# Loop heads of an attention kernel on the first slot of an instruction fetch block

## Chip, cores and metric

One Trainium2 chip, one core of it. The metric is the device time of one launch in microseconds (us), the median over several runs; lower is better. Four compute engines matter: TensorE (PE; its weight loads are listed as PEld), VectorE (DVE), ScalarE (ACT) and GpSimd (POOL). SyncE (SP) issues DMAs. Each engine runs its own instruction stream, and the streams meet at semaphores.

## What is computed

The input x is 4 x 2048 x 512 in float32. After a layernorm, `xn`, three things are added up:

```python
x = x + attention(xn) + tanh(xn @ weight @ aux_weight1 @ aux_weight2 + bias)
```

The attention has 16 heads of 32 channels: q, k and v from 512x512 weights with biases, `softmax(q k^T / sqrt(32)) v` over 2048 keys, and an output projection with its bias. With 4 batches there are 64 pairs of batch and head. They are called heads from here on, h = 0 to 63.

## The kernel before

The kernel has three stages, each in a block of its own. `build_weights` turns and multiplies the weights, `build_project` makes q, k, v and the tanh branch for 16 blocks of 512 tokens and stores them in DRAM, and `build_attend` works through the 64 heads and then makes the output projection. The projections and the scores hold their operands as a high and a low part, for accuracy; the stacks of three parts of 32 rows give the 96-row operands in the trace.

A head in `build_attend` has 16 key tiles (kt) of 128 keys and 4 query blocks (q) of 512, so 64 units.

- PE makes, for each unit, a tile of scores for the row maximum of the next head (`max_scores`, L837, into `sm_bank`) and a transposed tile of scores of this head (`scores`, L853, into one of three buffers of `st_bank`). After every second key tile it multiplies two finished tiles of exponentials by v (`use`, which calls `spread`, L859, into `pv_bank`). Once per head it adds up the softmax denominators (`add_up`, also L859, into `sum_bank`).
- DVE takes the row maxima out of `sm_bank` (`maxima`, L773).
- ACT takes the exponentials out of `st_bank` (`exps`, L695) and issues the DMAs that load q, k and v of the head three ahead (`load`, L210 for the q and k parts). With three buffers in `st_bank`, PE can be three units ahead of it.
- POOL adds ten of the sixteen tiles of exponentials in nine additions (`add`, L641), issues the five accumulating DMAs that add the other six (`join`, L652: 1 MB each, each waiting for the one before), and scales a result (`scale`, L659). The place of a tile of exponentials is used again once its addition or its join is done; ACT waits for that.
- SP spreads the reciprocals and stores the context.

What sets the order is written out by hand: `body(h, r, more, following)` of each engine handles key tiles 6 to 15 of head h and then key tiles 0 to 5 of head h + 1 (on POOL: the additions of head h + 1). The helper `heads` runs it. Its loop (`Fori`, the `with` line at L508) has 15 trips of four heads, r = 0 to 3, and the last four heads are written out behind the loop. The loop runs on each engine by itself, with a counter and a closing branch of its own, so an engine goes round without a barrier. [...] One trip holds about 2,660 instructions on PE, 715 on ACT, 540 on DVE, 190 on POOL and 100 on SP, register and wait instructions included and the two instructions of a matmul (weight load and matmul) counted as two. Before the loop, each engine's stream holds the other stages and the first pieces of head 0, so the loop's first instruction falls on whatever slot of a fetch block comes next.

Of the kernel before, what the change touches and what calls it, by code (L numbers as in the profile page):

```python
# [29 lines left out]
ALL_HEADS = BATCH * HEADS  # L30
GROUP = 4
# [421 lines left out]
def build_attend(nc, dram, out, first):  # L453
# [3 lines left out]
    with ExitStack() as own:  # L457
# [47 lines left out]

        def heads(eng, body):

            with nc.Fori(0, ALL_HEADS // GROUP - 1, engines=[eng.engine], hint_back_edge=True) as i:  # L508
                after = eng.snap(i + 1)
                for r in range(GROUP):  # L510
                    body(i * GROUP + r, r, GROUP, after * GROUP + (r + 1 - GROUP))
            for r in range(GROUP):
                body(ALL_HEADS - GROUP + r, r, GROUP - 1 - r, ALL_HEADS - GROUP + r + 1)
# [17 lines left out]
        def _(sp):  # L531
# [49 lines left out]
            def body(h, r, more, following):  # L581
# [16 lines left out]
                elif more == 1:  # L598
                    load_y(0, 0)

            heads(sp, body)
            store_result(1, 1)
            load_y(3, 1)
# [16 lines left out]
        def _(pool):  # L620
# [48 lines left out]
            def body(h, r, more, following):  # L669
                for i in range(POOL_ADDS):  # L670
                    if i == SCALE_ADD:
                        scale(h, r)
                    if more >= 1:
                        sum_up(following, (r + 1) % GROUP, i)

            heads(pool, body)

        @block.scalar
        def _(act):
# [45 lines left out]
            def body(h, r, more, following):  # L725
# [11 lines left out]
                else:  # L737
# [4 lines left out]
                    copy_sums(h, r)  # L742

            heads(act, body)
            for n in range(2, 4):
                high(n, n % 2)
# [255 lines left out]
```

## Time and profile before

| | us |
|---|---|
| time, median of 3 runs | 4283.07 (4282.47 to 4283.51) |
| profiled execution, its own time | 4286.54 |
| its span, first to last instruction | 4284.8 |
| PE busy | 4171.0 (97%) |
| POOL busy | 3185.7 (74%) |
| DVE busy | 2932.3 (68%) |
| ACT busy | 2361.2 (55%) |

The profile is of one execution. Its times count from the first instruction. "Busy" leaves out register, branch, wait and DMA-issuing instructions. An engine's name with a q (ACTq) is its sequencer. A wait put down to "issue" is one in which the engine waited for nothing that the profile shows. [...] Names such as `probs` and `sm_bank` are the program's; `probs` and `dma_sum` are both tiles of exponentials.

### The profile page before, as it was taken

The numbers are of one execution on the slowest core, as the hardware profiler recorded it, in microseconds if no ns is written. First come the engines' busy times: TensorE is split into PE (matmuls) and PEld (weight loads), VectorE is DVE, ScalarE is ACT, GpSimd is POOL, SyncE is SP. The second block draws the span as 40 slices with busy tenths as digits, with TensorE's granted clock in tenths as the row PEclk, the third lists the DMA queues.
The fourth block names the chain that finished last, engine by engine and source line by source line (L and its number), as shares of the span: only waits on it lengthen the run. The fifth ranks groups of instructions, "written<-read, shape, count | busy, mean of one in ns | idle before, by whom it ended". The sixth has DMA issues, their size and how long they took to land.

```text
span 4284.8 us, 77480 instructions
## 1 busy us (share of the span) xinstructions
PE 4171.0 (97%) x21728; PEld 2535.4 (59%) x21728; DVE 2932.3 (68%) x4928; ACT 2361.2 (55%) x4517; POOL 3185.7 (74%) x1119
## 2 busy tenths in 40 slices
PE   7999999999999999999999999999999999999999
PEld 5888888655555555555555555555555555555467
DVE  4344334488787777878777878787777878787434
ACT  2222222056676666666666667666666667666621
POOL 0322222279899999999999999999999999899930
PEclk9999999899999999999999999999999999999999
DMA  4444445357777777777777777777777777777677
GB/s 155 147 169 164 147 157 177 127 107 159 150 154 146 154 155 151 158 150 157 153 151 151 155 150 160 148 157 149 153 150 156 152 155 153 152 154 154 150 243 256
DMA packets 268281, 673.43 MB, mean 157 GB/s; under 512 B 109056, under 2 KB 110080, under 8 KB 214656
## 3 DMA queue, kind: packets, MB, share of 16 engines
q0 software_dynamic: 46080, 335.56, 41.1%
q1 hardware_dynamic: 138784, 220.26, 15.7%
q10 hardware_dynamic: 83040, 113.01, 9.5%
q8 instruction: 184, 3.01, 0.3%
q14 instruction: 193, 1.58, 0.1%
HBM read 195.30 MB, written 137.36 MB: 78 GB/s over the span
## 4 chain that ended last, share of the span: by engine, by line
PE 68%; issue 4%; POOL 3%; ACT 2%; DMA 2%; DVE 1%; ACTq 0%; POOLq 0%; DVEq 0%
PE pv_bank L859 21%; PE sm_bank L837 21%; PE st_bank L853 20%; POOL pool_sum L641 3%; PE sm_bank L200 3%; ACT probs L695 2%; PE sm_bank L859 2%; DMA dma_sum<-probs 1%; DVE part_max L773 1%; PE st_bank L200 1%; DMA q_stack<-max_row 1%; PE sm_bank L846 0%; DMA s_sums<-sum_copy 0%; POOL dma_sum L652 0%; ACTq L694 0%
## 5 line engine op out<-in xcount | busy, mean ns | idle before, releaser
L773 DVE TENSOR_REDUCE part_max<-sm_bank 128x1 f32<-128x512 f32 x4096 | 2498.4, 682 | 633.4 <-PE sm_bank L837 633.1
L641 POOL TENSOR_TENSOR pool_sum<-pool_sum,probs 128x2048 f32<-128x2048 f32 x512 | 2453.6, 4792 | 75.0 <-ACT probs L695 61.5
L695 ACT ACTIVATE probs<-st_bank 128x512 f32<-128x512 f32 x3840 | 1960.1, 617 | 679.5 <-PE st_bank L853 596.3
L853 PE MATMUL st_bank<-q_stack,k_stack 97*128 97x512 f32 x4096 | 1650.6, 404 | 66.3 <-ACT probs L695 58.4
L837 PE MATMUL sm_bank<-k_stack,q_stack 96*128 96x512 f32 x4096 | 1691.5, 417 | 11.4 <-DVEq L751 9.4
L837 PEld LDWEIGHTS sm_bank<-k_stack,q_stack 96*128 96x128 f32 x4096 | 786.9, 192 | 557.6 <-DVE part_max L773 323.4
L853 PEld LDWEIGHTS st_bank<-q_stack,k_stack 97*128 97x128 f32 x4096 | 780.4, 191 | 343.5 <-ACT probs L695 188.1
L859 PE MATMUL pv_bank<-probs,v_pair 128*32 128x512 f32 x7680 | 959.2, 615 | 0.0
L859 PEld LDWEIGHTS pv_bank<-probs,v_pair 128*32 128x32 f32 x7680 | 207.3, 111 | 467.7 <-ACT probs L695 274.0
L652 POOL DMA_DIRECT2D dma_sum<-probs x320 | 300.0, 938 | 150.8 <-DMA dma_sum<-probs 148.6
L312 POOL TENSOR_TENSOR y_out<-y_out,x_in 128x512 f32<-128x512 f32 x64 | 82.7, 1292 | 370.3 <-ACT y_out L341 364.4
L641 POOL TENSOR_TENSOR pool_sum<-probs 128x2048 f32<-128x2048 f32 x64 | 311.1, 4861 | 52.6 <-ACT probs L695 52.5
L385 DVE SCALAR_TENSOR_TENSOR qk_lo<-proj,qk_bias,qk_hi 128x512 fp32r<-128x512 f32 x128 | 96.2, 751 | 206.7 <-ACT qk_hi L335 205.0
L335 ACT ACTIVATE qk_hi<-proj,qk_bias 128x512 fp32r<-128x512 f32 x128 | 88.2, 689 | 264.8 <-PE proj L200 264.8
L695 ACT ACTIVATE dma_sum<-st_bank 128x512 f32<-128x512 f32 x256 | 132.5, 603 | 172.7 <-PE st_bank L853 172.7
L341 ACT ACTIVATE y_out<-y_out 128x512 f32<-128x512 f32 x64 | 40.5, 632 | 325.6 <-DVE y_out L407 325.6
L305 POOL TENSOR_TENSOR rstd<-rstd,power 128x4 f32<-128x4 f32 x16 | 16.3, 1018 | 260.2 <-DVE rstd L363 260.2
L200 PE MATMUL proj<-xt_hi,w_hi 128*128 128x512 f32 x512 | 203.7, 398 | 1.5 <-DVE xt_lo L375 1.5
L200 PE MATMUL proj<-w_hi,xt_lo 128*128 128x512 f32 x512 | 203.8, 398 | 0.0
L200 PE MATMUL proj<-xt_lo,w_hi 128*128 128x512 f32 x512 | 203.6, 398 | 0.0
L200 PE MATMUL proj<-xt_hi,w_lo 128*128 128x512 f32 x512 | 203.4, 397 | 0.0
L200 PE MATMUL proj<-w_hi,xt_hi 128*128 128x512 f32 x512 | 202.4, 395 | 0.0
(88 smaller groups left out, 2324.9 us busy)
## 6 DMA issues: line engine op xcount, KB each, us to landing
dma_sum<-probs POOLq DMA_DIRECT2D x320, 1024.0 KB, 8.5
q_stack<-s_q_hi ACTq DMA_DIRECT2D x122, 256.0 KB, 5.4
k_stack<-s_k_hi ACTq DMA_DIRECT2D x122, 256.0 KB, 5.2
x_in<-in_x SPq DMA_DIRECT2D x16, 1024.0 KB, 7.8
s_q_hi<-qk_hi SPq DMA_DIRECT2D x16, 1024.0 KB, 4.3
s_q_lo<-qk_lo SPq DMA_DIRECT2D x16, 1024.0 KB, 6.4
s_k_hi<-qk_hi SPq DMA_DIRECT2D x16, 1024.0 KB, 4.3
s_k_lo<-qk_lo SPq DMA_DIRECT2D x16, 1024.0 KB, 6.4
```

The source lines that it names most:

```text
L200: last = nc.tensor.matmul(out, a(c), b(c), start=(c == 0 and n == 0), stop=(c == CT - 1 and n == 2))
L312: nc.gpsimd.tensor_tensor(y_out[:, j], y_out[:, j], x_in[:, par, j], ALU.add).then_inc(half_y, 1)
L335: nc.scalar.activation(qk_hi[:, t, g], proj[:, u % RING], ACT.Identity, bias=keep["qk_bias"][:, t, g:g + 1]).then_inc(hi_ready, 1)
L341: nc.scalar.activation(y_out[:, j], y_out[:, j], ACT.Tanh).then_inc(tanh_ready, 1)
L385: nc.vector.scalar_tensor_tensor(qk_lo[:, t, g], proj[:, u % RING], keep["qk_bias"][:, t, g:g + 1], qk_hi[:, t, g].bitcast(F32), ALU.add, ...
L641: nc.gpsimd.tensor_tensor(total[:], one[:], tile_at(r, kt)[:], ALU.add).then_inc(pool_added, 1)
L652: nc.gpsimd.dma_start(dma_sum[c][r % 2][:], tile_at(r, CHAINS[c][j])[:], accum_op=ALU.add).then_inc(joined[c], DMA)
L695: nc.scalar.activation(tile_at(r, kt)[:, q * BLK:(q + 1) * BLK], st_bank[:, st_place(kt * QB + q)], ACT.Exp, scale=SCALE).then_inc(probs_r ...
L773: nc.vector.tensor_reduce(part_max[:, k:k + 1], sm_bank[:, sm_place(k)], AX.X, ALU.max).then_inc(max_scores_read, 1)
L837: nc.tensor.matmul(sm_bank[:, sm_place(k)], q_st[r][0:ROWS, q * P:(q + 1) * P], k_st[r][0:ROWS, b * BLK:(b + 1) * BLK], start=True, stop=T ...
L853: nc.tensor.matmul(st_bank[:, st_place(u)], k_st[r][0:ROWS + 1, kt * P:(kt + 1) * P], q_st[r][0:ROWS + 1, q * BLK:(q + 1) * BLK], start=Tr ...
L859: last = nc.tensor.matmul(bank[q * DH:(q + 1) * DH, :], left, right[:, q * BLK:(q + 1) * BLK], start=start, stop=stop)
```

## The change

The loop in `heads` gets one more argument. The library then pads each engine's stream ahead of the loop, so that the loop's first instruction is loaded at slot 0 of a fetch block. The padding is branched over, once, when the loop is entered. The body of the loop, its hint, its waits and the code behind it are the same instructions in the same order, only at other slots.

```diff
@@ build_attend, heads @@
 
         def heads(eng, body):
 
-            with nc.Fori(0, ALL_HEADS // GROUP - 1, engines=[eng.engine], hint_back_edge=True) as i:
+            with nc.Fori(0, ALL_HEADS // GROUP - 1, engines=[eng.engine], hint_back_edge=True,
+                         head_slot={eng.engine: 0}) as i:
                 after = eng.snap(i + 1)
                 for r in range(GROUP):
                     body(i * GROUP + r, r, GROUP, after * GROUP + (r + 1 - GROUP))
```

## Rows read from the trace of the kernel before

**Rows 1.** The page: span and engines

```profile
span 4284.8 us, 77480 instructions
PE 4171.0 (97%) x21728; PEld 2535.4 (59%) x21728; DVE 2932.3 (68%) x4928; ACT 2361.2 (55%) x4517; POOL 3185.7 (74%) x1119
```

**Rows 2.** The loop's own line, all trips: first and last start of each instruction

```profile
L508 PEldq BRANCH_PREFETCH_HINT  x15: 36/36/50, 888.8 to 3703.9; - x15
L508 ACTq BRANCH_PREFETCH_HINT  x15: 40/40/50, 888.8 to 3706.6; - x15
...
L508 PEldq COMPARE_BRANCH  x15: 88/357/387, 1084.1 to 3904.6; - x15
```

**Rows 3.** Stretches on PE: trip one, trip two, trip three

```profile
core 0: us, PE busy (x) PEld busy (x) DVE busy (x) ACT busy (x) POOL busy (x), PEclk, DMA share, GB/s
888.80:1084.10 195.30, 194.62 (x1088) 108.84 (x1084) 159.04 (x269) 134.88 (x265) 184.39 (x59) 1.00 0.73 155
1084.50:1285.90 201.40, 197.35 (x1096) 109.58 (x1092) 158.28 (x268) 134.96 (x264) 186.93 (x61) 0.98 0.73 153
1285.90:1488.00 202.10, 197.47 (x1100) 109.26 (x1092) 158.26 (x269) 134.93 (x264) 186.83 (x61) 0.98 0.73 153
```

**Rows 4.** Waits of ACT and of PE, loop (871 to 3910 us)

```profile
ACT probs L695 <- issue: 54.5, 14, 4.3
...
PE st_bank L853 <- ACT probs L695: 52.9, 16, 4.2
```

**Rows 5.** Waits of all engines, first trip (871 to 1084 us)

```profile
ACT probs L695 <- POOL pool_sum L641: 0.5, 1, 0.5
...
PE st_bank L853 <- ACT probs L695: 0.3, 2, 0.2
```

**Rows 6.** The loop's line around the second back-edge (1284 to 1294 us)

```profile
L508 ACTq COMPARE_BRANCH  x1: 59/59/59, 1288.7 to 1288.7; - x1
L508 ACTq BRANCH_PREFETCH_HINT  x1: 40/40/40, 1289.1 to 1289.1; - x1
```

**Rows 7.** Timeline of ACT behind that back-edge

```profile
1289.43 1.57 ACT L695 ACTIVATE probs<-st_bank 128x512 f32<-128x512 f32 x3 [0.25 <-PE st_bank L853]
1290.78 0.34 ACTq L210 DMA_DIRECT2D q_stack<-s_q_hi  x1
1290.88 0.62 ACT L695 ACTIVATE probs<-st_bank 128x512 f32<-128x512 f32 x1
1295.82 2.08 ACT L695 ACTIVATE probs<-st_bank 128x512 f32<-128x512 f32 x4 [4.32 <-issue]
```

**Rows 8.** Timeline of PE behind it; the last row is undisturbed, for comparison

```profile
1296.46 0.80 PE L853 MATMUL st_bank<-q_stack,k_stack 97*128 97x512 f32 x1 [4.19 <-ACT probs L695]
1297.19 3.64 PE L859 MATMUL pv_bank<-probs,v_pair 128*32 128x512 f32 x16
...
1267.13 1.92 PE L859 MATMUL pv_bank<-probs,v_pair 128*32 128x512 f32 x16
```

**Rows 9.** Stretches around that back-edge, with the granted clock

```profile
1280.00:1290.00 10.00, 9.93 (x63) 5.06 (x55) 6.09 (x11) 5.30 (x11) 10.00 (x4) 1.00 0.53 107
1290.00:1296.40 6.40, 2.28 (x10) 1.20 (x8) 3.86 (x7) 2.08 (x6) 6.32 (x2) 0.84 0.72 146
1296.40:1300.90 4.50, 4.43 (x18) 1.03 (x18) 0.00 (x0) 1.50 (x4) 4.29 (x3) 0.50 0.61 127
```

**Rows 10.** DMA queues in the second full trip of ACT (1288.7 to 1489.5 us)

```profile
q8 instruction: 11, 0.18, 0.4%
q14 instruction: 12, 0.10, 0.1%
```

**Rows 11.** DMA issues in the first trip: the joins

```profile
dma_sum<-probs POOLq DMA_DIRECT2D x20, 1024.0 KB, 8.5
```

**Rows 12.** Waits of POOL in the 14 later trips (1084 to 3906 us)

```profile
POOL dma_sum L652 <- DMA dma_sum<-probs: 128.9, 56, 4.0
POOL pool_sum L641 <- ACT probs L695: 58.9, 49, 3.5
```

**Rows 13.** Waits of ACT in the heads behind the loop (3906 to 4120 us)

```profile
ACT probs L695 <- issue: 1.9, 1, 1.9
ACT probs L695 <- POOL pool_sum L641: 1.8, 1, 1.8
```

**Rows 14.** Timeline of POOL around the second back-edge

```profile
1286.63 1.21 POOL L652 DMA_DIRECT2D dma_sum<-probs  x1
...
1305.90 4.59 POOL L641 TENSOR_TENSOR pool_sum<-pool_sum,probs 128x2048 f32<-128x2048 f32 x1 [3.29 <-ACT probs L695]
...
1331.81 0.88 POOL L652 DMA_DIRECT2D dma_sum<-probs  x1 [4.00 <-DMA dma_sum<-probs]
```

## The prediction

> **What bounds the kernel now.** The page comes first: PE is busy for 97% of the span and no other engine for more than 74% [rows 1]. In a kernel where PE alone is nearly full, moving instructions to other slots can save only what PE loses while it waits or while its clock is down. So the question is whether anything in the trace repeats with the loop.
>
> The second view is the line of the loop itself. The hint is the first instruction of a trip and the closing branch the last. On PE the first branch starts at 1084.1 us and the fifteenth at 3904.6 us [rows 2], so fourteen trips take 2820.5 us, or 201.46 us each. The first trip, entered from above and not by the branch, takes from 888.8 to 1084.1 us, 195.3 us, for the same body; with the 0.4 us that a taken branch needs on PE [rows 2] that is 195.7. Stretches cut at these times show the same: the clock is at 1.00 all through trip one and at 0.98 in trips two and three, and DVE, ACT and POOL have as much work in each [rows 3]. Every trip that is entered by the taken branch costs 5.8 us more than the one that is not.
>
> The third view says where. In the loop, ACT waits 14 times for "issue", 54.5 us in all, and PE waits 52.9 us for ACT's exponentials [rows 4]; 14 is the number of taken branches. In trip one the first of these is absent and the second is 0.3 us [rows 5]. The timeline behind the second back-edge gives the order: ACT's branch starts at 1288.7 and its hint runs at 1289.1 [rows 6], so the branch itself costs 0.4 us. ACT then does four exponentials and one DMA and stops until 1295.82, with 4.32 us of wait for nothing the trace shows [rows 7]. PE, at most three units ahead, stops with it: 4.19 us before its next score matmul. [...]
>
> What ACT waits for is, I think, its own instructions. Two queues carry only instructions, and in a trip they make 11 and 12 transfers, of 16 KB (0.18 MB / 11) and of 8 KB (0.10 MB / 12) [rows 10], so no engine that needs many of them keeps the loop. [...]
>
> [...] The trace puts 0.4 us at the branch and the long wait five operations behind it. [...]
>
> **The change part by part.** The head moves to slot 0 on five engines.
> - ACT: a whole block lies behind the branch instead of a remainder. Twelve loads of 8 KB a trip for some 1,250 instructions of ACT and DVE make a block some 105 instructions, about a seventh of ACT's trip, near 30 us, against the 6.8 us from hint to resumption (1289.1 to 1295.82). The wait goes, and with it PE's wait and the half clock: 5.8 us a trip if nothing else is late.
> - What is late next is POOL. In the fourteen later trips it waited 58.9 us for ACT [rows 12], nearly all of it right behind the back-edge (3.29 us in one piece, [rows 14]). That is 4.2 us a trip in which it caught up. Without it POOL's own trip is 201.46 - 4.2 = 197.25 us, of which 128.9 / 14 = 9.2 us are waits for its joins [rows 12]. ACT cannot write a tile of exponentials before POOL or a join has done with the old one, so a POOL that falls behind holds ACT, and PE with it. Bounds: 195.7 us a trip if POOL's lag stays free, 197.25 if POOL paces. In trip one, which had no rest for POOL either after its first additions, ACT was held for 0.5 us [rows 5]. I take 0.5 us over PE's pace, 196.2, because trip one is the nearest row.
> - DVE, POOL, SP: nothing waits for instructions in their streams now, and each keeps a first block longer than or equal to what it has. POOL's 190 and SP's 100 instructions are one or two blocks. Cost nothing; the cover is DVE's slack, 158 us busy in a trip of 201 [rows 3], and if its target came late PE would wait for its maxima as it now waits for ACT.
> - PE: the body is 2,660 instructions in 11 loads, ten full blocks and about 100 instructions, 7.6 us at the pace of the trip. [...] Nothing shows what this costs; from below it is 0; from above it is a join's 8.5 us less 7.6, 0.9, and as much again for the load itself, about 2 us. I take 0, since PE shows no such wait today, and keep the 2.
> - Entry: one taken branch over the padding per engine, 0.4 us once. The code behind the loop also moves; it has one such wait of 1.9 us on ACT [rows 13], which could go or double: plus or minus 2 us.
>
> The sum: 14 x (201.46 - 196.2) = 73.6, less 0.4, is 73.2 us. The profiled execution took 4286.54 us (span 4284.8), 3.5 us over the median; on it the sum gives 4213.3, and on the median of 4283.07 it gives **4210 us**.
>
> **The rivals.**
> - A, PE alone paces: 195.7 a trip, 80.7 - 0.4 saved, 4203 us. For it: ACT was held by POOL for only 0.5 us in trip one. Against it: the four last heads, which have no back-edge, show 1.8 us of that wait [rows 13].
> - B, POOL paces from the second trip on: 197.25, 59 us saved, 4224 us. For it, the 4.2 us of rest that disappear; against it, that a join's wait can shrink when POOL starts it at another time.
 Against it: today's branch on PE costs 0.4 us in every trip, with the same hint.
> - E, the wait has another cause (a fetch that every taken branch pays), or the head is not moved on ACT: 4283 us. [...]
>
> **How the numbers follow.** Forecast 0.46, A 0.18, B 0.16, C 0.08, D 0.04, E 0.08. The first four are faster, 0.88. A difference under 0.2% (8.6 us) can't be told from no change in this kernel; E lies there, 0.08, and D gives slower, 0.04. The range takes in A with 5 us for the code behind the loop and for trips that differ, 4198, and C nearly whole, 4236.
>
> **What would show it.** In the profile of the changed kernel: ACT's "issue" wait of 14 times gone or down to single ones; the branch-to-branch time on PE at 196 us instead of 201.5; the granted clock at 1.00 through the loop; PE's 3.64 us groups gone. For POOL: its wait for ACT shrinks from 58.9 us to under 20, and ACT's wait for POOL grows, little by the forecast, to over 10 us by B. C or D would show as PE starting its hint later than 0.4 us behind its branch. The prediction is wrong if a wait of over 3 us stays behind ACT's back-edge, or if PE's trip comes out above 198 us.

## The result, and the profile after

The changed kernel takes 4232.77 us (median of 4 runs, 4230.62 to 4234.31); the kernel before took 4282.77 us beside it (4 runs, 4275.68 to 4283.51). The ratio is 0.9884, with a 95% interval of [0.9873, 0.9896]; a bracket behind a ratio is this interval below too. It is faster by 50 us, where 73 us were forecast. The profiled execution took 4234.31 us, against 4286.54 us in the profile of before. In the fences below each line number behind line 508 is one higher than in the rows of before.

The page of the changed kernel, span and engines; they answer to [rows 1]. Below them is the page's part 4, the chain of work that ended last, by engine.

```profile
span 4232.5 us, 77485 instructions
PE 4144.6 (98%) x21728; PEld 2528.2 (60%) x21728; DVE 2932.1 (69%) x4928; ACT 2359.9 (56%) x4517; POOL 3189.9 (75%) x1119
...
PE 55%; DMA 9%; issue 7%; POOL 6%; ACT 3%; DVE 1%; POOLq 0%; ACTq 0%; SPq 0%; DVEq 0%
```

The same line of the page of the kernel before:

```profile
PE 68%; issue 4%; POOL 3%; ACT 2%; DMA 2%; DVE 1%; ACTq 0%; POOLq 0%; DVEq 0%
```

PE has 26 us less busy time, although it does the same 21,728 matmuls: the stretches at half clock (0.50 in [rows 9]) are gone. The chain runs through PE less, and more through transfers (9% where it was 2%) and through POOL (6% where it was 3%). That is the first sign of what paces the kernel now.

The loop's own line in the changed kernel, with instruction count, shortest, median and longest duration in ns, and first and last start; it answers to [rows 2]. The branch counts 16 because the entry is now a taken branch too.

```profile
L508 PEldq COMPARE_BRANCH  x16: 88/734/1908, 886.6 to 3846.0; - x16
...
L508 PEldq BRANCH_PREFETCH_HINT  x15: 36/36/50, 887.0 to 3649.9; - x15
```

The branches that close the trips start at 1084.7 us (first) and 3846.0 us (fifteenth) on PE, so the fourteen trips between them take 2761.2 us by the unrounded times, 197.23 us each instead of 201.46. The first trip is longer than it was, 1084.7 - 887.0 = 197.7 us against 195.3. And PE's branch itself, 0.36 us in the median before, now takes 0.73 us and up to 1.91 us.

Stretches on PE of the changed kernel (columns as in [rows 3]; PEclk is the clock granted to TensorE, as a share of the full one): trip one, the fourteen later trips, and the 20 us around the second back-edge, which answer to [rows 3, 9].

```profile
887.00:1084.70 197.70, 195.45 (x1096) 108.93 (x1092) 158.71 (x268) 134.57 (x264) 184.46 (x58) 1.00 0.72 153
1084.70:3845.90 2761.20, 2734.06 (x15284) 1522.36 (x15280) 2216.49 (x3752) 1887.37 (x3696) 2622.77 (x841) 1.00 0.74 156
1280.00:1300.00 20.00, 19.96 (x115) 10.35 (x113) 15.11 (x26) 13.17 (x27) 19.84 (x7) 1.00 0.70 140
```

The granted clock is 1.00 in all three. Around the back-edge, where PE was busy for 2.28 us of 6.4 and then ran at 0.50 [rows 9], it is now busy for 19.96 us of 20.

The timeline of ACT in the changed kernel behind the second back-edge, which answers to [rows 7]:

```profile
1285.13 1.57 ACT L696 ACTIVATE probs<-st_bank 128x512 f32<-128x512 f32 x3 [0.24 <-PE st_bank L854]
1286.49 0.34 ACTq L210 DMA_DIRECT2D q_stack<-s_q_hi  x1
1286.58 2.09 ACT L696 ACTIVATE probs<-st_bank 128x512 f32<-128x512 f32 x4
```

The three exponentials and the DMA are those of [rows 7]; the fourth exponential now runs on into the fifth, where ACT used to stand still for 4.32 us.

Waits in the fourteen later trips of the changed kernel (1084.7 to 3846 us): total us, times, longest. They answer to [rows 4, 12].

```profile
POOL dma_sum L653 <- DMA dma_sum<-probs: 116.6, 71, 4.5
...
PEld st_bank L854 <- DMA q_stack<-max_row: 24.7, 24, 1.5
PE st_bank L854 <- DMA q_stack<-max_row: 18.4, 26, 1.1
ACT probs L696 <- DMA dma_sum<-probs: 10.1, 7, 2.1
...
PE st_bank L854 <- ACT probs L696: 2.8, 4, 0.9
POOL pool_sum L642 <- ACT probs L696: 2.7, 4, 1.0
ACT probs L696 <- POOL pool_sum L642: 1.8, 1, 1.8
```

The same waits in the kernel before, over its fourteen later trips (1084.1 to 3905 us), those that [rows 4, 12] don't hold:

```profile
ACT probs L695 <- POOL pool_sum L641: 5.2, 3, 1.8
PEld st_bank L853 <- DMA q_stack<-max_row: 1.2, 3, 0.7
PE st_bank L853 <- DMA q_stack<-max_row: 0.4, 1, 0.4
```

ACT's 54.5 us of "issue" are gone altogether, PE's 52.9 us for ACT (52.6 of them in these trips) are down to 2.8, and POOL's 58.9 us for ACT to 2.7. One wait has come in their place: PE, and its weight loads, wait for `q_stack<-max_row`, 18.4 and 24.7 us where it was 0.4 and 1.2. That is the 8 KB transfer with which SP writes the next head's row of maxima into the query stack (`load_row`).

What such a wait looks like can be read in the changed kernel's timeline of POOL, SP and PE around one end of a head:

```profile
2933.09 0.88 POOL L653 DMA_DIRECT2D dma_sum<-probs  x1
2933.71 9.55 POOL L642 TENSOR_TENSOR pool_sum<-pool_sum,probs 128x2048 f32<-128x2048 f32 x2
...
2937.86 0.54 SPq L541 DMA_DIRECT2D q_stack<-max_row  x1
...
2943.20 0.86 POOL L653 DMA_DIRECT2D dma_sum<-probs  x1
...
2944.40 0.50 PE L854 MATMUL st_bank<-q_stack,k_stack 97*128 97x512 f32 x1 [0.86 <-DMA q_stack<-max_row]
```

POOL issues the third join of a head at 2933.09; by the trace it lands 9.3 us later. SP issues the row 4.8 us behind it, while the join is under way, and PE, whose next scores need the row, gets it at 2944.40, 6.5 us after its issue and 0.86 us too late. Meanwhile POOL makes two additions, 9.55 us, and issues the fourth join at 2943.20.

Put together, on PE's own marks: 14 x (201.46 - 197.23) = 59.2 us are won in the later trips, 2.4 us lost in the first and 6.4 us behind the loop (386.5 us from the last branch to the end, against 380.1). A rest of 1.8 us was won ahead of the loop. Together that is 52.2 us, against 52.3 us between the two spans.

### The profile page after: what moved, and what is told of

Read it like the earlier page. It is cut to its first block, busy times and chain, and to the rows that moved or that the text cites. A ratio compares the mean times of both kernels' runs of the same rounds, so it can differ in the third digit from the quotient of the medians.

```text
span 4232.5 us, 77485 instructions
## 1 busy us (share of the span) xinstructions
PE 4144.6 (98%) x21728; PEld 2528.2 (60%) x21728; DVE 2932.1 (69%) x4928; ACT 2359.9 (56%) x4517; POOL 3189.9 (75%) x1119
## 4 chain that ended last, share of the span: by engine, by line
PE 55%; DMA 9%; issue 7%; POOL 6%; ACT 3%; DVE 1%; POOLq 0%; ACTq 0%; SPq 0%; DVEq 0%
PE pv_bank L860 17%; PE sm_bank L838 16%; PE st_bank L854 16%; POOL pool_sum L642 5%; DMA dma_sum<-probs 5%; DMA q_stack<-max_row 3%; ACT probs L696 3%; PE sm_bank L200 2%; PE sm_bank L860 2%; DVE part_max L774 1%; PE st_bank L200 1%; DMA q_stack<-s_ctx 0%; PE sm_bank L847 0%; POOL dma_sum L653 0%; DVE max_row L758 0%
## 5 line engine op out<-in xcount | busy, mean ns | idle before, releaser
L860 PE MATMUL pv_bank<-probs,v_pair 128*32 128x512 f32 x7680 | 935.4, 602 | 0.0
```

The costliest lines, as they stand in the source:

```text
L860: last = nc.tensor.matmul(bank[q * DH:(q + 1) * DH, :], left, right[:, q * BLK:(q + 1) * BLK], start=start, stop=stop)
```

## The experiments

The times below were each taken beside the kernel before. "Trip" is the mean of the fourteen later trips on PE and "branch gaps" the sum over them of the time from PE's branch to the hint behind it; both are worked out from the loop's line, and were 201.46 and 6.0 us before and 197.23 and 15.7 us after. All edits are made to the changed kernel.

### Which engine's slot does it

ACT alone aligned:

```diff
-                         head_slot={eng.engine: 0}) as i:
+                         head_slot={eng.engine: 0} if eng.engine == mybir.EngineType.Activation else None) as i:
```

> Only ACT's loop head is put on slot 0; the other four keep the slots of the kernel before. Theory (ACT ran out of its block behind the branch, and joins and row loads pace what is left): the wait for issue behind ACT's back-edge is gone, the trip on PE is 197.2 us as with all five aligned, PE's branch is back at 0.36 us median instead of 0.73, the time is 4233 us, within 5 us. Rival (another engine's alignment carries part of it): the time stays above 4250 us.

Measured: 4217.86 us (4215.12 to 4220.05), ratio 0.9839 [0.9823, 0.9855]; trip 196.80, branch gaps 6.1, 379.7 us behind the loop. Every engine but ACT aligned (the two arms of the condition swapped):

> Slot 0 for PE, DVE, POOL and SP, while ACT's head keeps its old slot. Theory: the 3.9 us wait behind each of ACT's fourteen back-edges stays, and the time is that of the kernel before, 4283 us, up to 10 us more for PE's slower branch. Rival: under 4270 us.

Measured: 4282.99 us, 0.9996 [0.9987, 1.0006]; trip 200.95, branch gaps 16.6.

Waits of ACT in the later trips (1085 to 3900 us) with all engines but ACT aligned:

```profile
ACT probs L696 <- issue: 44.2, 13, 4.2
```

So the whole gain is ACT's. The four other engines bring none, and together with ACT they take away 15 us of it, which neither theory had: both had ACT alone at about 4233 us or above. ACT alone was run once more, beside the last experiment below:

> The kernel with ACT's head alone at slot 0 once more, in more rounds and beside the two above: 4218 us. If the 15 us to the kernel with all five aligned were chance, it comes out at 4225 to 4233 us.

Measured: 4218.25 us (4216.3 to 4223.45), 0.9852 [0.9839, 0.9866]; trip 196.69. Its interval lies clear of that of all five (0.9873 to 0.9896), so the 15 us stand. It is the fastest version here that computes everything.

### Is it the length of ACT's first block

ACT's head at slot 111, the others at 0:

```diff
-                         head_slot={eng.engine: 0}) as i:
+                         head_slot={eng.engine: 111 if eng.engine == mybir.EngineType.Activation else 0}) as i:
```

> All heads at slot 0 but ACT's at slot 111, 17 slots ahead of a multiple of 128. If ACT's blocks hold 128 instructions (8 KB), it runs dry after 17 instructions and the wait of some 3.9 us comes back fourteen times: trip 201.5 us, time 4283 to 4290 us. If its blocks hold 256 instructions, 145 slots are left, over 30 us of work, and the time is that of all at slot 0, 4233 us.

Measured: 4282.06 us, 0.9985 [0.9973, 0.9997]; trip 201.18.

Timeline of ACT behind the second back-edge, with ACT's head at slot 111:

```profile
1288.64 0.34 ACTq L210 DMA_DIRECT2D q_stack<-s_q_hi  x1
1288.72 0.62 ACT L696 ACTIVATE probs<-st_bank 128x512 f32<-128x512 f32 x1
1292.40 2.08 ACT L696 ACTIVATE probs<-st_bank 128x512 f32<-128x512 f32 x4 [3.06 <-issue]
```

ACT's wait in its later trips (1085 to 3900 us) in the same kernel:

```profile
ACT probs L696 <- issue: 38.3, 12, 4.2
```

The stall of the kernel before is back, at the same operation and at nearly the same cost (201.18 us a trip, 201.46 before). The theory with blocks of 128 had said so, 201.5 us. In a block of 256 instructions slot 111 would leave 145 of them behind the head, more than the 32 that were enough at slot 96 below, and nothing would happen; so the run decides for blocks of 128, of which 17 are left. Such a block goes with the transfers of 8 KB: 12 of them a trip for some 1,250 instructions of ACT and DVE [rows 10], some 105 each by the prediction's estimate, where blocks at the ends of a trip need not be used whole.

When is the block behind the target asked for: as the engine enters the target's block, or once that is used up? ACT's head at slot 96 leaves 32 instructions:

```diff
-                         head_slot={eng.engine: 0}) as i:
+                         head_slot={eng.engine: 96 if eng.engine == mybir.EngineType.Activation else 0}) as i:
```

> All heads at slot 0 but ACT's at 96, with 32 slots left in its block instead of 17. Undisturbed, ACT reaches the 32nd instruction 6.5 us behind its hint, and in the kernel before it went on 6.8 us behind it. Theory: the wait shrinks to 0.5 us or nothing, no half clock, trip 197.2 to 197.5 us, 4233 to 4238 us. Rival (the next block is asked for only when the block is used up): the wait of 3.9 us stays, 4283 us.

Measured: 4233.06 us, 0.9884 [0.9869, 0.9899]; trip 197.63. From 871 to 3860 us ACT has no "issue" wait at all, where it had 12 (38.3 us) with its head at slot 111. If the fetch began only at the block's last instruction, the wait would have been there at slot 96 too. So it begins earlier, and 32 instructions of ACT's work cover it.

### Does PE's short last block cost the rest

PE's 2,660 instructions a trip go with 11 transfers of 16 KB [rows 10]; at ACT's 8 KB for 128 instructions each holds 256, an estimate. By it, with PE's head at slot 128, its last block in the loop has some 230 instructions instead of some 100:

```diff
-                         head_slot={eng.engine: 0}) as i:
+                         head_slot={eng.engine: 128 if eng.engine == mybir.EngineType.PE else 0}) as i:
```

> PE's head at slot 128, the others at 0. PE's last block then holds 231 instructions ahead of the branch instead of 103, some 17 us instead of 7.6. Theory (the load of the target sometimes comes late behind a join): PE's branch falls from a median of 0.73 us to 0.36 us. Whether the time follows tells who paces the trip: PE, then some 0.4 us a trip less, 6 us in all, 4227 us; joins and row loads, then no change, 4233 us.

Measured: 4236.41 us (4230.07 to 4244.51), 0.9891 [0.987, 0.9911]; trip 197.33, branch gaps 5.9. The times spread over 14 us, so a few us either way would not show in them.

The loop's line on PE, with PE's head at slot 128:

```profile
L508 PEldq COMPARE_BRANCH  x16: 88/357/391, 888.6 to 3846.6; - x16
```

Waits in its later trips (1085 to 3838 us):

```profile
POOL dma_sum L653 <- DMA dma_sum<-probs: 108.8, 67, 3.5
...
ACT probs L696 <- DMA dma_sum<-probs: 18.7, 9, 2.7
PE st_bank L854 <- DMA q_stack<-max_row: 14.1, 23, 1.3
```

PE's branch is back to 0.36 us, and the 9.8 us that it had gained in gaps are gone. The trip and the time have not moved. So PE's late branch was real and cost nothing that can be measured. That PE would otherwise have waited for the row of maxima instead fits these rows, but is argued and not shown by itself.

### What paces the trip now

The joins are the 1 MB accumulating transfers that POOL issues, and POOL waits for them. If their length has a part in the pace, halving them frees it; if PE's own work set it, nothing would move. This kernel leaves out half of the columns in every sum that a join makes:

```diff
-                nc.gpsimd.dma_start(dma_sum[c][r % 2][:], tile_at(r, CHAINS[c][j])[:],
+                nc.gpsimd.dma_start(dma_sum[c][r % 2][:, :SEQ // 2], tile_at(r, CHAINS[c][j])[:, :SEQ // 2],
```

> All five heads at slot 0; the five joins of a head move half of each tile, 512 KB instead of 1 MB, so the other half of those sums is left out. Theory (the joins' durations pace POOL, and their traffic delays the row loads): the trip on PE falls from 197.2 us to PE's own 195.7 to 196.1 us, PE's waits for the row load (46 us in the loop) fall under 10 us, the time is 4205 to 4215 us. Rival (POOL's own additions pace): the trip stays above 196.8 us.

Measured: 4193.89 us, 0.9786 [0.9769, 0.9804]; trip 195.16, first trip 194.1, 375.8 us behind the loop.

DMA issues of the kernel with half joins, later trips (1086 to 3830 us): count, KB each, median us from issue to landing.

```profile
dma_sum<-probs POOLq DMA_DIRECT2D x281, 512.0 KB, 4.9
q_stack<-max_row SPq DMA_DIRECT2D x56, 8.0 KB, 2.0
```

Its waits (1085 to 3838 us):

```profile
POOL pool_sum L642 <- ACT probs L696: 90.3, 57, 2.0
POOL dma_sum L653 <- DMA dma_sum<-probs: 10.4, 13, 1.3
```

The same two DMA issues in the changed kernel (1086 to 3830 us):

```profile
dma_sum<-probs POOLq DMA_DIRECT2D x279, 1024.0 KB, 8.6
q_stack<-max_row SPq DMA_DIRECT2D x56, 8.0 KB, 5.4
```

With joins of 4.9 us PE no longer waits for the row of maxima (the row is in none of its waits), POOL again waits for ACT instead of for its joins, and the trip is 195.16, under the 195.7 that stood in the prediction for PE's own pace. The time is 11 us below the lower end of what was expected. The 8 KB row takes 5.4 us to land beside 1 MB joins and 2.0 us beside halved ones. The edit takes away two things at once, POOL's waits for joins and the late row, so by itself it does not tell which of them paced; the next two kernels look at them one by one.

Rival B had POOL pace by its own work. Then less addition would speed it up. This kernel adds only half the columns in one of POOL's additions of each head, and leaves out the other half:

```diff
-                nc.gpsimd.tensor_tensor(total[:], one[:], tile_at(r, kt)[:], ALU.add).then_inc(pool_added, 1)
+                w = slice(0, SEQ // 2 if i == 5 else SEQ)
+                nc.gpsimd.tensor_tensor(total[:, w], one[:, w], tile_at(r, kt)[:, w], ALU.add).then_inc(pool_added, 1)
```

> All five heads at slot 0; the sixth of POOL's nine additions adds half the columns, so a part of the sum is left out and POOL has about 2.3 us a head less to do; the joins stay whole. Theory (POOL's additions plus joins are one chain that paces the trip): the chain is 9 us a trip shorter, POOL waits for ACT again, the trip falls to 195.7 to 196.1 us and the time to 4205 to 4215 us. Rival (the row load alone paces, because any join in flight delays it): PE's waits for the row load stay over 25 us in the loop and the trip above 196.8 us.

Measured: 4227.41 us, 0.9865 [0.9848, 0.9883]; trip 197.35, first trip 194.1.

Waits in its later trips (1085 to 3838 us):

```profile
POOL dma_sum L654 <- DMA dma_sum<-probs: 241.9, 111, 4.5
...
PE st_bank L855 <- DMA q_stack<-max_row: 15.9, 26, 1.1
```

Its timeline of POOL between a third and a fourth join, one addition narrow:

```profile
2930.30 7.35 POOL L643 TENSOR_TENSOR pool_sum<-pool_sum,probs 128x1024 f32<-128x1024 f32 x2
2939.96 0.88 POOL L654 DMA_DIRECT2D dma_sum<-probs  x1 [2.31 <-DMA dma_sum<-probs]
```

A miss. The addition became shorter and the trip did not: POOL's wait for its joins grew from 116.6 to 241.9 us and swallowed what was freed. But this shows less than that POOL's additions don't matter, for the addition that was narrowed is one of the two that run beside the third join, the longest (9.9 us in the mean). In the changed kernel, over the later trips, the five stretches from one join's issue to the next take 10.46, 10.09, 10.54, 8.53 and 9.70 us in the mean, 49.3 us a head. In the first, second and fifth POOL waits for next to nothing (0.01 us): its additions fill them. Ahead of the fourth join it waits 0.39 us for the third, and ahead of the fifth 1.79 us for the fourth. With the narrow addition the wait ahead of the fourth join is 2.60 us, and the stretch 10.58; the other four are unchanged within 0.02 us. So additions and joins stand one behind the other in POOL's round, and an addition that a join hides cannot shorten it. Whether a shorter addition in one of the other three stretches would, no run tried. The rival of that expectation, that the late row alone paces, had both its signs here: PE and its weight loads still waited 37 us for the row, and the trip was above 196.8.

Is the row of maxima only in the way, so that asking for it earlier wins the time? It is asked for four units of maxima earlier with

```diff
-TURN_UNIT = 8
+TURN_UNIT = 4
```

> All five heads at slot 0; the row of maxima is turned at unit 4 of the next head instead of unit 8, so its 8 KB load starts about one key tile (3 us) earlier, and nothing else changes. If the late row load is what paces PE: the waits for it vanish and the trip falls to 196.0 us or less, time 4215 us. If POOL and the joins pace and the row load only hands it on: the waits for the row vanish too, but waits of ACT for joins and additions take their place, and the trip stays at 197 us, time 4233 us.

Measured: 4247.92 us, 0.9906 [0.9886, 0.9926]; trip 198.43.

Waits in its later trips (1085 to 3838 us):

```profile
ACT probs L696 <- DMA dma_sum<-probs: 40.2, 28, 2.3
PE st_bank L854 <- DMA q_stack<-max_row: 3.0, 6, 0.7
```

The wait for the row is nearly gone, and nothing is won: by the ratios the kernel is 9 us slower than with the row at unit 8, with intervals that touch, and its trip is 1.2 us longer. Neither theory had it slower. ACT now waits 40.2 us for joins to release tiles, 10.1 before. The 1.2 us lie in one place: the stretch from the third join to the fourth has grown from 10.54 to 10.87 us, four times a trip, and the third join from 9.87 to 10.24 us. So the late row alone is not the cause; take its wait away and ACT's wait for POOL's round holds PE instead. That the row had only passed on POOL's pace to PE fits this, but is argued. With ACT alone aligned as well the same edit gave the same picture:

> Only ACT's head at slot 0, and the row turned at unit 4. With the first theory (row load paces): 196.0 us a trip instead of 196.8, time 4207 us. With the second (joins pace): 4218 us, as with ACT's head alone.

Measured: 4241.29 us, 0.9891 [0.9874, 0.9909]; trip 198.88, and ACT's wait for joins 47.5 us (29 times) from 1085 to 3838 us, where it was 6.4 with ACT alone aligned. Here the intervals lie apart (0.9839 and 0.9852 without the edit): it costs some 20 us.

The last attempt was to take a transfer out of the joins' way. The load of the values, 512 KB in ACT's stream twice a trip, was moved from key tile 15 to key tile 8:

```diff
-LOAD_AT = [6, 7, 9, 10, 12, 13, 15]
+LOAD_AT = [6, 7, 9, 10, 12, 13, 8]
```

> All five heads at slot 0; ACT issues the 512 KB load of v, twice a trip, at key tile 8 instead of 15, so that it runs beside the second join and not beside the fourth. Theory (joins pace, and the fourth, which the fifth waits for at once, is slowed to 10 us by the load of v where it otherwise takes 7.2): in the two heads of a trip with that load the fourth join falls under 8.5 us, POOL's wait for joins falls from 128 us to under 100, the trip from 197.2 to 196.0 us, the time to 4212 us. Rival (another join is slowed by as much): trip and time unchanged.

Measured: 4352.82 us, 1.0165 [1.0151, 1.0179]; trip 204.41. And with ACT alone aligned:

> Only ACT's head at slot 0, and the load of v at key tile 8. Theory: trip from 196.8 to 195.9 us, time from 4218 to 4203 us. Rival: 4218 us.

Measured: 4368.07 us, 1.02 [1.0186, 1.0214]; trip 206.24. Both misses by a wide margin.

Waits in the later trips (1085 to 3900 us) of the kernel with the early load, all engines aligned:

```profile
POOL pool_sum L642 <- ACT probs L696: 173.2, 115, 3.3
ACT probs L696 <- issue: 95.0, 20, 5.1
POOL dma_sum L653 <- DMA dma_sum<-probs: 54.3, 55, 2.1
```

Its timeline of ACT in one such place:

```profile
1101.20 0.41 ACTq L216 DMA_DIRECT2D v_pair<-s_v  x1
...
1103.13 3.91 ACTq L210 DMA_DIRECT2D q_stack<-s_q_hi  x1
...
1107.29 1.57 ACT L696 ACTIVATE probs<-st_bank 128x512 f32<-128x512 f32 x3 [3.35 <-PE st_bank L854]
```

The issuing instruction of these loads over the whole kernel (shortest, median, longest ns), with the early load:

```profile
L210 ACTq DMA_DIRECT2D q_stack<-s_q_hi x122: 322/323/5637, 891.0 to 3964.4; - x122
```

and in the changed kernel:

```profile
L210 ACTq DMA_DIRECT2D q_stack<-s_q_hi x122: 317/322/369, 890.7 to 3858.4; - x122
```

The joins did what was hoped: the fourth of a head, the one meant, takes 7.15 us in the mean instead of 7.96, all of them 7.7 in the median instead of 8.6, and POOL's wait for them halved. But the next load in ACT's stream is now issued 1.9 us behind the values' load (23 us before), and ACT's sequencer is held in the very instruction that issues it: over 1 us behind every one of the 31 loads of the values, 3.91 us here and 5.64 at most, where 0.32 is usual. The 95.0 us of "issue" in fourteen trips are 6.8 us a trip, and the trip is 7.2 us longer. PE waits behind ACT, and its mean granted clock falls to 0.976 over the span, from 0.989. The timeline also warns of a label: ACT's gap at 1107.29 is put down to PE, though by these rows ACT's own sequencer stood until 1107.04.

## Why the prediction was right or wrong

The time lies in the range, 3 us below its upper end, and on the side that was forecast, but the gain was a third smaller than forecast, 50 us for 73. That it still lies in the range is in part luck: the room at the upper end had been kept for rival C, PE's late branch, which cost nothing measurable, and three other things filled it, a pace of 197.23 instead of 196.2 us, a longer first trip and a longer tail.

**The cause of the 5.8 us**: right. ACT ran out of its short first block. PE waited 52.9 / 14 = 3.8 us for it at a back-edge, in the mean, and behind the second one it then ran at a clock of 0.50, which cost 3.64 - 1.92 = 1.7 us on sixteen matmuls and 0.4 us on a score matmul of 0.80 us [rows 4, 8, 9]. With the block long enough the three went together, and putting the head near a block's end (slot 111) brought them back: ACT's "issue" wait with 38.3 us, PE's wait for ACT with 41.0 us, both from 1085 to 3900 us, and a clock of 0.50 from 1293 to 1297 us. Rival E falls with the first experiments.

**The step that failed** is the second bullet, POOL late next, "I take 0.5 us over PE's pace, 196.2". The trip is 197.23 us, 1.0 us more; over fourteen trips that is 14.4 us. By the spans of the two profiled executions 20.9 us are missing (73.2 - 52.3). The value was taken from trip one as the nearest row. In trip one a POOL that falls behind has not yet held anybody for long (0.5 us); in the later trips it no longer has the 4.2 us of rest in which to catch up, which the same paragraph had found and priced at 197.25. POOL's wait for ACT went from 58.9 to 2.7 us. So the choice between the bounds was wrong, and the upper bound was met to 0.02 us.

**Rival B** named that pace, 4224 us, and its mechanism in the main: a POOL without rest, additions and joins one behind the other. The 0.02 us are luck, though. Its working took the waits for joins, 9.2 us a trip, as fixed; they shrank to 8.3, and POOL's busy time and "issue" waits grew by 0.5 us between them, the small rest beside its rows making up the difference. How POOL's lateness reaches PE was named in part. B expected ACT held by POOL for over 10 us; the row for POOL's additions is 1.8 us, with the waits for its joins it is 11.9, where it was 5.2. The larger share comes to PE by the row of maxima, 18.4 us, which no rival had.

**Trip one and the code behind the loop** were given nothing and plus or minus 2 us. They cost 2.4 and 6.4 us, together 8.8 us; with the 14.4 that is 23.2, less 2.2 ahead of the loop (1.8 won where 0.4 was to be paid), which makes the 20.9 to 0.1. The first of the two differs from kernel to kernel: trip one took 195.1 us with PE at slot 128 and 195.2 with ACT at 96, so its 2.4 us may be chance. Behind the loop these two have 381.7 and 383.8 us, over 380.1 both. Behind the loop (3846 to 4067 us) the waits of ACT are these:

```profile
ACT probs L696 <- DMA dma_sum<-probs: 6.1, 3, 3.4
ACT q_stack L714 <- POOL ctx_out L660: 4.2, 1, 4.2
...
ACT probs L696 <- issue: 3.1, 1, 3.1
```

The issue wait was 1.9 us [rows 13], a change inside the plus or minus 2. The wait for joins was absent there before, and the one for `ctx_out` was 0.5 us. A POOL that leaves the loop with a greater lag, so that the tail has to wait for it, was not thought of; that this is the cause is argued from these rows and not tested.

**Rival C** showed itself and did not count. PE starts its hint 0.48 to 1.97 us behind its branch, close to the 2 us of its upper bound, 9.7 us more in all; with PE's head at 128 they are gone, at the same time within the intervals. Its price assumed 2 us at every branch, and that PE paces. **Rival D** would have needed 3.8 us at that branch; the longest is 1.97. The prices of both took it that the target's block is loaded while PE works through its last block, and that such a load waits for a join, 8.5 us. That was the author's estimate: no run shows when a load of instructions starts or how long it takes, nor what the hint does for it, as every kernel here has the hint. What the runs showed in its place is the branch on PE, 0.73 us in the median with some 100 instructions in the last block and 0.36 us with some 230, and another small transfer, the 8 KB row, which took 5.4 us beside 1 MB joins. D's 2.0 us for the lowered clock are the 1.7 and 0.4 above. **DVE, POOL and SP at nothing**: not confirmed. ACT alone is 15 us faster than all five, 14 x 0.5 = 7 us in the trips (196.80 and 196.69 against 197.23) and 6.8 or 8.9 us behind the loop (379.7 and 377.6). PE's branch does not explain it, since PE at 128 does not bring it back. In the trips it shows in the same stretch as above: POOL's wait for the third join is 0.26 and 0.21 us a head instead of 0.39, and that stretch 10.40 and 10.35 us instead of 10.54. Which of the other engines' slots, or which shift of the code behind the loop, takes it was not tried, and stays open.

## What to carry to other kernels

Compare the first trip of a loop with the later ones: the same body with 5.8 us more in each trip that was entered by a branch is a cost of the branch, and a wait for "issue" at the same operation each time tells on which engine. Try the alignment on the engine that shows it alone as well, here ACT: alone it gave 67 and 64 us, with the others 50. Before booking the whole of a stall that goes, price the trip for the engine that used the stall to catch up, and where its waits are for long transfers, take that price. And before narrowing an operation as a test of who paces, look whether a transfer runs beside it that is longer: then the test says nothing of the other operations.

## What the runs showed of the hardware

- With ACT's loop head at slot 111 the stall behind the back-edge was there (12 "issue" waits, 38.3 us; trip 201.18 us), at slots 0 and 96 it was not (none; 197.23 and 197.63 us). By blocks of 128 instructions (8 KB), the reading that fits these runs, the block behind the target's was late with 17 instructions left in the target's block and in time with 32.
- The 8 KB row, which SP issues, took 5.4 us in the median to land beside POOL's 1 MB joins (8.6 us) and 2.0 us beside joins of 512 KB (4.9 us).
- An instruction that issues a DMA took 3.91 us, and up to 5.64, where it followed the load of the values by 1.9 us on the same queue, against 0.32 us elsewhere; it was over 1 us in 31 of 31 such places. ACT's next exponential stood still for it, 3.35 us, and the timeline put that down to PE.
- PE's head at slot 0 left some 100 instructions in its last block (the estimate above), and the branch took 0.73 us in the median and up to 1.91 us, against 0.36 and up to 0.39 us in the kernel before; with the head at slot 128 and some 230 instructions it took 0.36 and up to 0.39 us again.
